# Mixture-of-experts stage on tokens sorted by expert, through DRAM, in place of all four experts on every token

## The chip, the cores and the metric

The kernel runs on one core of a Trainium2 chip. The metric is the device time of one execution in microseconds (us), lower is better. The engines are TensorE (PE, with its weight loads PEld), VectorE (DVE), ScalarE (ACT), GpSimd (POOL) and SyncE (SP); SP, ACT and POOL issue DMAs, which run on 16 shared DMA engines.

## The reference, cut to what matters

A residual stream `x` of 32 x 128 = 4096 tokens with 128 features passes through eight sublayers. Only the second half of the last one changes:

```python
x = x + mla_attention(rmsnorm(x, norm1_w), ...)
n = rmsnorm(x, norm2_w)
top = argmax(n @ gate_w.T + gate_b)                  # one expert of 4 for each token
h = relu(einsum('btd,ehd->bteh', n, W1) + b1)         # 128 -> 512 hidden
y = einsum('bteh,edh->bted', h, W2) + b2              # 512 -> 128
x = x + y[chosen expert]
```

All matmuls of these sublayers are in float32.

## The kernel before, in words

The program is a list of phases; every engine runs its own instruction list, and `phase_end` (line 971) is a barrier of all five engines after each phase. Within a phase, work is pipelined over the 32 items (an item is 128 tokens) with written-out lags (`steps`), and semaphores order the engines.

Phase 1 is the first attention, during which SP loads the weights of all layers (`late_loads`, line 2023). The phase "latent" (lines 1620 to 1760) makes queries, keys and values of the last attention, in two loops: 32 items with a 320-column matmul (line 1733), then 16 pairs. In the first loop ACT has three operations per item: `take_rows` (line 998), `take_z` (line 1697, the stream that goes on) and `take_latent` (line 1694). Phase "L4" is the last attention; POOL cuts the causal triangle out of the probabilities there (`cut`, line 518) and copies v (line 507).

The last phase is the expert stage, in 8 groups of 512 tokens. For each group: scale by the inverse root mean square (L1789), transposition (L1890), `norm2` (L1794), gate matmuls (L1896), the choice of the expert as a one-hot (L1804 to L1811). The one-hot is transposed and spread over partitions, so that each of four masks has a value per token (L1901, L1908, L1819). Then all four experts run on all 512 tokens: 16 chunks of "up" (L1916: weights 128x128, 512 moving columns), Relu with bias on ACT and DVE in turns (L1875, L1851), 16 chunks of "down" (L1938). DVE multiplies each expert's result by its mask and sums (`combine`, L1826, L1830); the sum is transposed back (L1922), added to the stream (L1837) and stored by SP (L2160). `up` runs two chunks ahead of `down`, and the next group's preparation is spread between the chunks, so that PE always has a matmul at hand:

```python
for c in range(CHUNKS):                               # 16
    ... nc.tensor.matmul(ps[:, 4 + e % 2, :], w_down[:, c, :], hid[:, c % 4, :], ...)
    if c + 2 < CHUNKS: up(i, k, c + 2)
```

## Time and profile before

| | us |
|---|---|
| median of 3 runs | 1413.96 (1412.5 to 1418.36) |
| span of the profiled execution | 1414.9 |
| PE busy / PEld busy | 1260.0 / 841.6 |
| DVE / ACT / POOL busy | 919.3 / 591.5 / 273.6 |
| expert stage, from L2171 to the last store | 1146.08 to 1414.9 |

The span runs from the first to the last instruction of one execution, which the profiler recorded; for that execution the profile gives no other time than this span. PE's matmuls are pipelined, so that the times from one start to the next say more than the durations of single instructions. A float32 matmul appears as two instructions.

### The profile page before, as it was taken

What the parts mean: (1) busy time and instruction counts of PE and PEld (TensorE: products, weight loads), DVE (VectorE), ACT (ScalarE), POOL (GpSimd) and SP (SyncE); (2) the same over time, 40 slices, a digit from 0 to 9 for tenths busy, and PEclk for the clock granted to TensorE, in tenths of its full rate; (3) what the DMA queues carried; (4) which work ended last, traced back from release to release, by engine and by line L of the source; (5) the groups of instructions that cost most, each with busy time, mean ns of one, the idle gap of its engine ahead of it and who ended that gap; (6) DMA issues with size and microseconds to landing.
All of it is one profiled execution on the core that took longest, in us unless ns stands there. A gap on an engine that the chain in (4) does not pass through costs nothing. (4 is left out here: it accounts for less than half of the span.)

```text
span 1414.9 us, 36612 instructions
## 1 busy us (share of the span) xinstructions
PE 1260.0 (89%) x13819; PEld 841.6 (59%) x13819; DVE 919.3 (65%) x2730; ACT 591.5 (42%) x1343; POOL 273.6 (19%) x766
## 2 busy tenths in 40 slices
PE   3999988938849997999898998799999959999998
PEld 2888876735437773444456886447888734444443
DVE  4778849976455875999423886756777645555554
ACT  2788845641234663222343554753444411111111
POOL 0222211220402330000000221434554500000000
PEclk9999998967977998999897999877999969999999
DMA  9500000000000003000000000010000000000000
GB/s 287 138 4 3 3 2 1 2 1 1 1 0 2 3 3 120 1 1 1 1 1 1 3 3 2 1 60 2 3 3 3 3 1 8 8 7 7 7 7 16
DMA packets 27076, 25.59 MB, mean 18 GB/s; under 512 B 6176, under 2 KB 22944, under 8 KB 26656
## 3 DMA queue, kind: packets, MB, share of 16 engines
q1 hardware_dynamic: 25904, 23.17, 5.5%
q8 instruction: 112, 1.84, 0.5%
q14 instruction: 52, 0.43, 0.1%
q10 hardware_dynamic: 1008, 0.16, 0.1%
HBM read 21.23 MB, written 2.10 MB: 16 GB/s over the span
## 5 line engine op out<-in xcount | busy, mean ns | idle before, releaser
L703 PE MATMUL ps<-kT,qTm 32*128 32x128 f32 x3200 | 252.4, 293 | 0.8 <-DVE kT L408 0.8
L671 PE MATMUL ps<-qTm,kT 32*128 32x512 f32 (+1 forms) x1024 | 250.8, 554 | 2.4 <-ACT probs L574 2.1
L703 PEld LDWEIGHTS ps<-kT,qTm 32*128 32x128 f32 x3200 | 228.3, 204 | 6.1 <-issue 2.6
L1938 PE MATMUL ps<-kv_all,ctx_all 128*128 128x512 f32 x256 | 134.1, 605 | 5.3 <-DVE kv_all L1851 5.3
L1875 ACT ACTIVATE kv_all<-ps,b_col 128x512 f32<-128x512 f32 x64 | 44.0, 687 | 215.9 <-PE ps L1916 215.9
L1916 PE MATMUL ps<-q_all,ctx_all 128*128 128x512 f32 x256 | 132.3, 599 | 0.0
L380 DVE TENSOR_REDUCE neg_max<-ps 128x8 f32<-128x1024 f32 x72 | 87.9, 1221 | 60.6 <-PE ps L703 60.6
L574 ACT ACTIVATE probs<-ps 128x1024 f32<-128x1024 f32 x72 | 73.7, 1024 | 121.0 <-PE ps L713 121.0
L1851 DVE TENSOR_SCALAR kv_all<-ps,b_col 128x512 f32<-128x512 f32 x64 | 48.0, 750 | 116.3 <-PE ps L1916 116.3
L860 PE MATMUL ps<-probs,v_wide 128*32 128x128 f32 x3200 | 116.9, 280 | 4.6 <-DVE o_sb L429 1.7
L671 PEld LDWEIGHTS ps<-qTm,kT 32*128 32x128 f32 x1024 | 85.5, 190 | 49.4 <-issue 40.2
L499 POOL CAST nm<-neg_max 128x16 bf16<-128x16 f32 (+1 forms) x132 | 26.8, 203 | 428.6 <-DVE neg_max L367 160.9
L375 DVE TENSOR_REDUCE neg_max<-ps 128x4 f32<-128x512 f32 x128 | 82.2, 684 | 33.2 <-PE ps L703 33.2
L394 DVE TENSOR_TENSOR qTm<-ps,hmask 128x512 f32<-128x512 f32 (+1 forms) x132 | 73.2, 555 | 37.7 <-ACT nmT L552 20.6
L713 PE MATMUL ps<-nmT,sel_max 32*128 32x128 bf16 x1600 | 95.9, 219 | 0.0
L570 ACT ACTIVATE probs<-ps,bias_col 128x512 f32<-128x512 f32 x128 | 80.9, 683 | 35.4 <-PE ps L713 35.4
L1529 PE MATMUL ps<-tap_w,xqT 128*128 128x512 f32 x192 | 93.6, 624 | 0.0
L860 PEld LDWEIGHTS ps<-probs,v_wide 128*32 128x32 f32 x3200 | 80.8, 111 | 19.6 <-issue 6.5
L1916 PEld LDWEIGHTS ps<-q_all,ctx_all 128*128 128x128 f32 x256 | 49.1, 192 | 61.3 <-issue 61.3
L564 ACT ACTIVATE probs<-ps,bias_col 128x1024 f32<-128x1024 f32 x64 | 71.3, 1114 | 32.5 <-PE ps L713 32.5
L827 PE MATMUL ps<-pv_pick,pv 128*128 128x72 f32 (+1 forms) x528 | 82.0, 278 | 0.9 <-ACT pv L580 0.9
L580 ACT ACTIVATE pv<-ps 128x256 f32<-128x256 f32 x132 | 50.6, 383 | 71.2 <-PE ps L860 71.2
(375 smaller groups left out, 2600.8 us busy)
## 6 DMA issues: line engine op xcount, KB each, us to landing
ctx_all<-in_ctx SPq DMA_DIRECT2D x4, 1024.0 KB, 10.5
ctx_all<-in_ctxT SPq DMA_DIRECT2D x2, 2048.0 KB, 10.5
x_all<-in_x SPq DMA_DIRECT2D x4, 512.0 KB, 7.0
out<-x_all SPq DMA_DIRECT2D x8, 256.0 KB, 2.3
ctx_all<-in_W1T SPq DMA_DIRECT2D x1, 1024.0 KB, 5.3
tap_w<-in_conv_wT SPq DMA_DIRECT2D x1, 768.0 KB, 7.0
w_l<-in_w SPq DMA_DIRECT2D x2, 256.0 KB, 3.4
above<-in_c_above SPq DMA_DIRECT2D x1, 256.0 KB, 3.4
```

The costliest lines, as they stand in the source:

```text
L375: nc.vector.tensor_reduce(neg_max[:, k, per * g:per * g + per], ps[:, raw_bank(L, b, g), 0:N].rearrange("p (h k) -> p h k", h=per), AX.X, ...
L380: nc.vector.tensor_reduce(neg_max[:, k, H2 * u:H2 * u + H2].rearrange("p (a h) -> p a h", a=2), ps[:, 4 * u:4 * u + 2, 0:N].rearrange("p a ...
L570: nc.scalar.activation(probs[:, k % 2, N * g:N * (g + 1)], ps[:, final_bank(L, b, g), 0:N], ACT.Exp, bias=bias).then_inc(sem("probs_ready" ...
L574: nc.scalar.activation(probs[:, k % 2, 2 * N * u:2 * N * (u + 1)].rearrange("p (a n) -> p a n", a=2), ps[:, 2:4, 0:N], ACT.Exp, bias=bias) ...
L671: nc.tensor.matmul(ps[:, bank, at:at + N], kT[rows_of(g), k, :], qTm[rows_of(g), k, 0:N], start=True, stop=False, skip_group_check=True)
L703: last = nc.tensor.matmul(dst, qTm[rows_of(g), k, 128 * i:128 * i + 128], kT[rows_of(g), k, :], start=False, stop=True, skip_group_check=True)
L713: last = nc.tensor.matmul(dst, sel_max[rows_of(g), i, :], nmT[rows_of(g), k, :], start=False, stop=True, skip_group_check=True)
L827: last = nc.tensor.matmul(ps[:, 7, 256 + W * half:256 + W * half + W], pv[:, k % 2, 128 * half:128 * half + 128], pv_pick[:, 0 if heads == ...
L860: last = nc.tensor.matmul(ps[32 * j:32 * j + 32, 7, 128 * half:128 * half + 128], v_tile(k % 2, heads, 4 * half + j, i), probs[:, k % 2, 1 ...
L1529: last = nc.tensor.matmul(dst, xqT[:, k % 2, tap:tap + 128], tap_w[:, tap, :], start=False, stop=tap == 2)
L1916: nc.tensor.matmul(ps[:, c % 2, :], w_up[:, c, :], xm_T[:, k, :], start=True, stop=True).then_inc(sem("mo_hidden"), 1)
L1938: nc.tensor.matmul(ps[:, 4 + e % 2, :], w_down[:, c, :], hid[:, c % 4, :], start=c % 4 == 0, stop=c % 4 == 3).then_inc(sem("mo_down"), 1)
```

## The change

The four experts no longer run on all tokens. In the latent phase the gate weights are appended to the 320-column weights as four more columns, and to the output projection of the last attention, so that the logits arrive in `z_all[:, b, 128:132]` beside the stream (one more small ACT copy per item). In L4 POOL also adds stream and residual into the right half of a record per token (`keep_rest`). A record has 257 words: normalised row, rest, token number.

The last phase then does this. DVE works out the expert, and a place for each token, from 20-odd small operations and two small matmuls. The places of one expert are consecutive, in a region of 4096 rows in a new DRAM tensor `places`. POOL scatters the 32 items' records to DRAM by 32 indirect DMAs of 128 records each. SP waits for all of them, and loads tiles of 512 records. Eleven tiles (8 + 3, enough for any split of the tokens) each run one expert, whose weights and biases (128 rows of 1156 words) POOL fetches by an indirect DMA. Four indirect DMAs per tile scatter the result rows of 512 B to the output; places without a token carry a number out of bounds, which is skipped. Tiles are held in 4 buffers, results and weights in 3. `places` (16,896 rows of 1028 B, 17.4 MB) is filled with empty records at the start, by one DMA of SP behind the loads of phase 1. Gone are the mask and its spreading, the constant `sel` (L1427), the loads of all experts (L2153) and the plain store.

The diff, cut to its core (in `mixture_vector` the choice and the places are left out; `mixture_*` take the places of `expert_*` and `store`):

```diff
+TILE_ROWS = 512
+N_TILES = B * S // TILE_ROWS + N_EXP3 - 1
+TILE_SLOTS = 16
+RECORD = 2 * D + 1
+REGION = B * S
+SPARE = N_EXP3 * REGION
+NO_TOKEN = 1 << 20
+EXPERT_ROW = 2 * HID + HID // 128 + D
...
+            def keep_rest(b, k):
+                pool.wait_ge(*after("x_updated", b + 1))
+                nc.gpsimd.tensor_tensor(records[:, b, D:2 * D], x_all[:, b, :], z_all[:, b, 0:D], ALU.add)
...
+            if L == "L4":
+                work += [(9, keep_rest)]
...
-            nc.scalar.activation(sel[:], sel_col[:].unsqueeze(2).broadcast_to([128, 16, 128]), ACT.Copy)
...
-            nc.scalar.activation(w_h1[:], w_h1[:], ACT.Copy, scale=col("norm1")).then_inc(sem("la_weights"), 1)
-            act.wait_ge(sem("la_centred"), 1)
-            nc.scalar.activation(w_h1[:], ps[:, 6, 0:320], ACT.Copy).then_inc(sem("la_weights"), 1)
+            nc.scalar.activation(w_h1[:, 0:320], w_h1[:, 0:320], ACT.Copy, scale=col("norm1")).then_inc(sem("la_weights"), 1)
+            nc.scalar.activation(w_h1[:, 320:320 + N_EXP3], gate_w[:], ACT.Copy, scale=col("norm2")).then_inc(sem("la_weights"), 1)
+            act.wait_ge(sem("la_centred"), 2)
...
             def take_latent(b, k):
                 act.wait_ge(sem("la_halves"), b + 1)
+                nc.scalar.activation(z_all[:, b, D:Z], ps[:, 2 + k, 320:320 + N_EXP3], ACT.Copy, scale=inv_ln[:, b:b + 1])
...
-            nc.tensor.matmul(ps[:, 6, 0:320], centre[:], w_h1[:], start=True, stop=True).then_inc(sem("la_centred"), 1)
+            pe.wait_ge(sem("la_weights"), 2)
+            nc.tensor.matmul(ps[:, 7, 0:N_EXP3], w_o3_nat[:], w_h1[:, 320:320 + N_EXP3], start=True, stop=True
+                             ).then_inc(sem("la_centred"), 1)
+            nc.tensor.matmul(ps[:, 6, 0:320 + N_EXP3], centre[:], w_h1[:], start=True, stop=True
+                             ).then_inc(sem("la_centred"), 1)
...
                 wait_reuse(pe, after("la_raw"), b, RING)
-                nc.tensor.matmul(ps[:, 2 + k, 0:320], rowT[:, k % 2, :], w_h1[:], start=True,
+                nc.tensor.matmul(ps[:, 2 + k, 0:320 + N_EXP3], rowT[:, k % 2, :], w_h1[:], start=True,
...
+        def stored_after(engine, j):
+            if j >= 0:
+                engine.wait_ge(sem("mx_stored_%d" % (j % 3)), 64 * (j // 3 + 1))
+        def mixture_sync(sp):
+            sp.wait_ge(sem("mx_tiled"), 1)
+            for j in range(N_TILES):
+                row = sp.value_load(tile_row[0:1, j:j + 1], min_val=0, max_val=SPARE)
+                if j == 0:
+                    sp.wait_ge(sem("mx_placed_rows"), 16 * B)
+                stored_after(sp, j - 4)
+                sp.dma_start(tile_of(j), places[bass.ds(row, TILE_ROWS), :].rearrange("(k p) c -> p k c", p=128)
+                             ).then_inc(sem("mx_loaded_%d" % (j % 4)), 16)
+            for j in range(N_TILES - 3, N_TILES):
+                stored_after(sp, j)
+        def mixture_gpsimd(pool):
+            G = nc.gpsimd
+            G.memset(restart, 1.0).then_inc(sem("mx_restart"), 1)
+            G.tensor_copy(records[:, :, 2 * D:RECORD].bitcast(I32), token_id[:].unsqueeze(2)).then_inc(sem("mx_ids"), 1)
+            pool.wait_ge(sem("mx_restart"), 1)
+            G.memset(by_expert(restart)[:, :, 0:1], 0.0).then_inc(sem("mx_restart"), 1)
+            def fetch(j):
+                G.indirect_dma_start(out=expert_of(j), out_offset=None, in_=t_in["experts"],
+                                     in_offset=bass.IndirectOffsetOnAxis(ap=weight_id[:, j:j + 1], axis=0)
+                                     ).then_inc(sem("mx_weights_%d" % (j % 3)), 16)
+            pool.wait_ge(sem("mx_ids"), 1)
+            pool.wait_ge(sem("places_cleared"), 16)
+            pool.wait_ge(sem("mx_placed"), 1)
+            for b in range(B):
+                pool.wait_ge(sem("mx_rows"), b + 1)
+                G.indirect_dma_start(out=places, out_offset=bass.IndirectOffsetOnAxis(ap=place_id[:, b:b + 1], axis=0),
+                                     in_=records[:, b, :], in_offset=None).then_inc(sem("mx_placed_rows"), 16)
+                if b == 8:
+                    pool.wait_ge(sem("mx_tiled"), 1)
+                    for j in range(3):
+                        fetch(j)
+            for j in range(N_TILES):
+                pool.wait_ge(sem("mx_result"), j + 1)
+                for k in range(4):
+                    G.indirect_dma_start(out=out_rows_2d, out_offset=bass.IndirectOffsetOnAxis(
+                                             ap=tile_of(j)[:, k, 2 * D:RECORD].bitcast(I32), axis=0),
+                                         in_=result_of(j)[:, 128 * k:128 * k + 128], in_offset=None,
+                                         bounds_check=B * S - 1, oob_is_err=False
+                                         ).then_inc(sem("mx_stored_%d" % (j % 3)), 16)
+                if j + 3 < N_TILES:
+                    fetch(j + 3)
...
+        def mixture_scalar(act):
+            act.wait_ge(sem("mx_inv"), 1)
+            for b in range(B):
+                nc.scalar.activation(records[:, b, 0:D], z_all[:, b, 0:D], ACT.Copy, scale=inv_all[:, b:b + 1]
+                                     ).then_inc(sem("mx_rows"), 1)
+            for j in range(N_TILES):
+                relu_free(act, j)
+                for c in (0, 2):
+                    act.wait_ge(sem("mx_up"), 4 * j + c + 1)
+                    nc.scalar.activation(hidden_of(j, c), ps[:, 2 + c, :], ACT.Relu, bias=b_up(j, c)
+                                         ).then_inc(sem("mx_relu_even"), 1)
...
+            def take_features(j):
+                dve.wait_ge(sem("mx_turned"), j + 1)
+                if j >= 2:
+                    dve.wait_ge(sem("mx_up"), 4 * (j - 1))
+                V.tensor_scalar(features_of(j), ps[:, j % 2, :], col("norm2"), None, ALU.mult
+                                ).then_inc(sem("mx_features"), 1)
+            def relu(j):
+                relu_free(dve, j)
+                for c in (1, 3):
+                    dve.wait_ge(sem("mx_up"), 4 * j + c + 1)
+                    V.tensor_scalar(hidden_of(j, c), ps[:, 2 + c, :], b_up(j, c), 0.0, ALU.add, ALU.max
+                                    ).then_inc(sem("mx_relu_odd"), 1)
+            def add_bias(j):
+                rest = tile_of(j)[:, :, D:2 * D]
+                q.count(V.tensor_tensor(rest, rest, b_down(j).unsqueeze(1).broadcast_to([128, 4, D]), ALU.add))
+            def finish(j):
+                dve.wait_ge(sem("mx_down"), j + 1)
+                stored_after(dve, j - 3)
+                q.end()
+                V.tensor_tensor(result_of(j).rearrange("p (k d) -> p k d", k=4),
+                                ps[:, 6 + j % 2, :].rearrange("p (k d) -> p k d", k=4), tile_of(j)[:, :, D:2 * D], ALU.add
+                                ).then_inc(sem("mx_result"), 1)
+            take_features(0)
+            take_features(1)
+            relu(0)
+            for j in range(N_TILES):
+                add_bias(j)
+                if j + 2 < N_TILES:
+                    take_features(j + 2)
+                if j + 1 < N_TILES:
+                    relu(j + 1)
+                finish(j)
...
+            pe.wait_ge(sem("mx_chosen"), 1)
+            nc.tensor.matmul(ps[:, 0, 0:128], upperb[:], one_hot, start=True, stop=True)
+            nc.tensor.matmul(ps[:, 1, 0:128], onesb[:], one_hot, start=True, stop=True).then_inc(sem("mx_counted"), 1)
+            def turn(j):
+                pe.wait_ge(sem("mx_loaded_%d" % (j % 4)), 16 * (j // 4 + 1))
+                if j >= 2:
+                    pe.wait_ge(sem("mx_features"), j - 1)
+                for k in range(4):
+                    last = nc.tensor.transpose(ps[:, j % 2, 128 * k:128 * k + 128], tile_of(j)[:, k, 0:D], ident[:])
+                last.then_inc(sem("mx_turned"), 1)
+            def up(j):
+                pe.wait_ge(sem("mx_features"), j + 1)
+                pe.wait_ge(sem("mx_weights_%d" % (j % 3)), 16 * (j // 3 + 1))
+                for c in range(4):
+                    if j:
+                        pe.wait_ge(sem("mx_relu_odd" if c % 2 else "mx_relu_even"), 2 * (j - 1) + c // 2 + 1)
+                    nc.tensor.matmul(ps[:, 2 + c, :], w_up(j, c), features_of(j), start=True, stop=True
+                                     ).then_inc(sem("mx_up"), 1)
+            def down(j):
+                pe.wait_ge(sem("mx_relu_even"), 2 * j + 2)
+                pe.wait_ge(sem("mx_relu_odd"), 2 * j + 2)
+                if j >= 2:
+                    pe.wait_ge(sem("mx_result"), j - 1)
+                for k in range(4):
+                    for c in range(4):
+                        last = nc.tensor.matmul(ps[:, 6 + j % 2, 128 * k:128 * k + 128],
+                                                hidden_of(j, c)[:, 128 * k:128 * k + 128], w_down(j, c),
+                                                start=c == 0, stop=c == 3)
+                last.then_inc(sem("mx_down"), 1)
+            turn(0)
+            turn(1)
+            up(0)
+            for j in range(N_TILES):
+                if j + 2 < N_TILES:
+                    turn(j + 2)
+                if j + 1 < N_TILES:
+                    up(j + 1)
+                down(j)
...
+            sp.wait_ge(sem("empty_set"), 2)
+            sp.dma_start(places.rearrange("(p r) c -> p r c", p=128),
+                         empty_row[:].unsqueeze(1).broadcast_to([128, (SPARE + TILE_ROWS) // 128, RECORD])
+                         ).then_inc(sem("places_cleared"), 16)
...
-        def expert_loads(sp):
-            sp.dma_start(w_up.rearrange("p (e c) h -> p e (c h)", e=N_EXP3), t_in["W1T"].rearrange("e d n -> d e n")).then_inc(sem("experts_loaded"), 16)
-            sp.dma_start(w_down, t_in["W2T"].rearrange("e (c h) d -> h (e c) d", h=128)).then_inc(sem("experts_loaded"), 16)
-            sp.wait_ge(sem("experts_loaded"), 32)
```

## Rows read from the trace of the kernel before

**Rows 1.** First lines of the profile's page: busy us, share, instructions.

```profile
span 1414.9 us, 36612 instructions
PE 1260.0 (89%) x13819; PEld 841.6 (59%) x13819; DVE 919.3 (65%) x2730; ACT 591.5 (42%) x1343; POOL 273.6 (19%) x766
```

**Rows 2.** A stretch of the expert stage: length, busy time of each engine, clock, DMA.

```profile
1250.00:1300.00 50.00, 48.09 (x157) 23.27 (x156) 27.62 (x56) 8.24 (x12) 2.53 (x2) 1.00 0.04 10
```

**Rows 3.** Groups by line in the expert stage: busy us, mean ns, idle before.

```profile
L1938 PE MATMUL ps<-kv_all,ctx_all 128*128 128x512 f32 x256 | 134.1, 605 | 5.3 <-DVE kv_all L1851 5.3
L1916 PE MATMUL ps<-q_all,ctx_all 128*128 128x512 f32 x256 | 132.3, 599 | 0.0
...
L1851 DVE TENSOR_SCALAR kv_all<-ps,b_col 128x512 f32<-128x512 f32 x64 | 48.0, 750 | 116.3 <-PE ps L1916 116.3
...
L1830 DVE TENSOR_TENSOR kv_all<-kv_all 128x512 f32<-128x512 f32 x24 | 16.6, 692 | 4.0 <-DVE kv_all L1826 3.4
```

**Rows 4.** Chain of waits, expert stage: start, us, engine, line, count.

```profile
1301.87 0.86 PE ps L1916 x2
```

**Rows 5.** Timeline, end of L4 and expert stage: start, us, engine, line, idle before.

```profile
1142.49 0.29 DVE L436 TENSOR_TENSOR ctx_all<-ctx_all,ps 128x128 f32<-128x128 f32 x1 [0.95 <-PE ps L783]
...
1145.76 0.19 DVE L241 SCALAR_TENSOR_TENSOR inv_all<-moment,inv_all 128x32 f32<-128x32 f32 x1
...
1157.74 3.59 PE L1916 MATMUL ps<-q_all,ctx_all 128*128 128x512 f32 x4
...
1164.60 0.60 PE L1890 MATMUL ps<-ident,kv_all 128*128 128x128 f32 x4
...
1168.47 0.95 PE L1896 MATMUL ps<-gate_w,q_all 128*128 128x4 f32 x8
```

**Rows 6.** DMA issues: size, median us from issue to landing.

```profile
x_all<-in_x SPq DMA_DIRECT2D x4, 512.0 KB, 7.0
out<-x_all SPq DMA_DIRECT2D x8, 256.0 KB, 2.3
ctx_all<-in_W1T SPq DMA_DIRECT2D x1, 1024.0 KB, 5.3
```

**Rows 7.** Timeline of SP's DMA issues at the start: start, us, count.

```profile
5.36 9.75 SPq L2019 DMA_DIRECT2D ctx_all<-in_ctx  x4
...
35.25 0.42 SPq L2029 DMA_DIRECT2D above<-in_c_above  x1
...
70.90 0.59 SPq L2029 DMA_DIRECT2D cols<-in_ln_b  x1
```

**Rows 8.** Timeline of the latent phase's first loop.

```profile
895.05 0.25 ACT L1694 ACTIVATE ctx_all<-ps 128x64 f32<-128x64 f32 x1
895.15 0.31 ACT L998 ACTIVATE rowT<-ps 128x128 f32<-128x128 f32 x1
...
895.71 0.25 ACT L1694 ACTIVATE ctx_all<-ps 128x64 f32<-128x64 f32 x1
...
915.97 1.43 ACT L1708 ACTIVATE o_sb<-ctx_all 128x64 f32<-128x64 f32 x4 [1.61 <-DVEq L1658]
```

**Rows 9.** POOL's timeline in L4, and its adder in the latent phase.

```profile
895.21 0.46 POOL L1675 TENSOR_TENSOR q_all<-probs 128x128 f32<-128x128 f32 x1 [0.19 <-DVE ctx_all L1633]
...
1043.40 1.09 POOL L518 TENSOR_SCALAR_AFFINE_SELECT probs<-probs 128x1024 f32<-128x1024 f32 x1 [0.41 <-PE ps L776]
...
1046.64 0.20 POOL L499 CAST nm<-neg_max 128x16 bf16<-128x16 f32 x1 [2.15 <-DVE neg_max L380]
```

**Rows 10.** Two early stretches, columns as in Rows 2.

```profile
20.00:35.00 15.00, 11.01 (x79) 8.92 (x81) 6.59 (x13) 5.67 (x20) 0.57 (x3) 1.00 1.07 304
...
50.00:70.00 20.00, 20.00 (x422) 17.49 (x420) 15.76 (x34) 16.79 (x44) 4.81 (x20) 1.00 0.46 122
```

**Rows 11.** Timeline, the end of phase 1, and the copy of `sel`.

```profile
201.54 0.21 DVE L220 TENSOR_TENSOR moment<-stats_all 128x32 f32<-128x32 f32 x1 [0.43 <-SPq L971]
...
393.11 1.89 ACT L1427 ACTIVATE sel<-sel_col 128x2048 bf16<-128x2048 f32 x1
```

More of the change, by code:

```diff
@@ L121, with build @@
 BIASES = ("L0", "L2", "L3")
-def build(nc, t_in, out):
+TILE_ROWS = 512
[6 more added lines that the diff above has]
+EXPERT_ROW = 2 * HID + HID // 128 + D
+def build(nc, t_in, out, places):
     with ExitStack() as ctx_:
@@ L1768, in build @@
-        chosen = work_m[:, 4096:8192].rearrange("p (k e t) -> p k e t", k=2, e=4)
-        xm_T = q_all[:, 0:8, :].rearrange("p a b -> p (a b)").rearrange("p (k t) -> p k t", k=2)
-        def loop_groups(engine, body):
-            body(0, 0)
-            with engine.Fori(0, GROUPS // 2 - 1) as pair:
-                for u in range(2):
-                    body(pair * 2 + (u + 1), (u + 1) % 2)
-            body(GROUPS - 1, 1)
-        def is_last(i):
-            return isinstance(i, int) and i == GROUPS - 1
@@ L1869, in expert_scalar @@
-        def expert_scalar(act):
-            def group(i, k):
-                for c in range(0, CHUNKS, 2):
-                    act.wait_ge(sem("mo_hidden"), i * CHUNKS + (c + 1))
-                    if c >= 4 or not is_first(i):
-                        act.wait_ge(sem("mo_down"), i * CHUNKS + (c - 3))
-                    nc.scalar.activation(hid[:, c % 4, :], ps[:, c % 2, :], ACT.Relu,
-                                         bias=b1_col[:, c:c + 1]).then_inc(sem("mo_relu_even"), 1)
-            loop_groups(act, group)
@@ L2282, in constants @@
     up, none = np.arange(1, SLOTS + 1), np.full(SLOTS, -1)
-    sel = np.zeros((128, 16))
-    for i in range(16):
-        sel[3 * i:3 * i + 3, i] = sel[64 + 3 * i:64 + 3 * i + 3, i] = 1
     row = t % 32
@@ L2346 @@
     out = nc.dram_tensor("out_0", (B, S, D), F32, kind="ExternalOutput").ap()
-    build(nc, t_in, out)
+    places = nc.dram_tensor("places", (SPARE + TILE_ROWS, RECORD), F32).ap()
+    build(nc, t_in, out, places)
     got = run_bass_kernel_spmd(nc, [{"in_" + n: a for n, a in arrays.items()}], core_ids=[0])
```

306 lines of the change are left out of this document (118 added, 188 removed).

## The prediction, made before the changed kernel ran

> **What bounds the kernel now.** I read the page's first lines, then the busy time by stretches, then the groups by line of the last phase, then its timeline. The page gives a span of 1414.9 us with PE busy for 89% of it [rows 1]. In the expert stage PE is the only engine without slack: in a 50 us stretch it is busy 48.09 us at full clock, DVE 27.62 and ACT 8.24 [rows 2]. The groups by line say with what: 266.4 us of summed durations are the 128 "up" and 128 "down" matmuls [rows 3]. One matmul of 512 columns takes 0.86 us of PE from start to start (its two instructions) [rows 4], so 256 of them are 220 us of the 268.9 us from the end of the moments, 1145.95 us [rows 5], to the end of the span. No DMA ends a wait there. The stage is bound by matmul work of which three quarters are masked away.
>
> **What the change takes away.** All of that stage: 268.9 us. What it puts in its place is a prologue that PE only waits for, and eleven tiles. I build the new end from 1145.95 us, within the profiled execution.
>
> **Side costs before the stage.** In the latent loop ACT starts the same operation every 0.66 us (895.05, 895.71), back to back, so it has no room [rows 8]. The added copy of four columns has the form of L1694, which holds the next one up by 0.10 us (895.05 to 895.15); from above, the copies with scale and bias take 1.43/4 = 0.36 us each [rows 8]. I take 0.17, nearer to the like row, since a scale per partition comes with it: 32 x 0.17 = 5.4 us (3.2 to 11.5). The two small copies and the small matmul ahead of the loop I put at 0.7 us. POOL's `keep_rest` is a 128x128 add, 0.46 us [rows 9], in a step of L4 with gaps of 0.41 and 2.15 us on POOL; the cut behind it is then late by some 0.1 us, and its reader on PE runs a step later. Hidden; only the last one shows at the barrier, 0.4 us. If that cover were gone, it costs 32 x 0.46 = 15 us. The four more columns in L4's products cost nothing that can be seen. Dropping the copy of `sel` gains between 0 and its 1.89 us [rows 11]; I take 0. Together +6.5: the stage starts at 1152.5 us.
>
> **The cleared places.** 17.4 MB are written from about 71.5 us, behind the last load [rows 7]. At the 304 GB/s of the loads at 20 to 35 us [rows 10] that is 57 us; at the 114 GB/s that 256 KB landing in 2.3 us give [rows 6], 153 us, to 224 us. The first barrier that SP shares falls at about 201.5 us [rows 11]. So it costs 0 down to 135 GB/s, and 23 us at worst. PE was busy all through 50 to 70 us with the DMA engines 46% busy [rows 10], so I put instruction fetches beside the clearing at 0, 10 us at worst.
>
> **Routing.** Seven DVE operations, each waiting for the one before, two small matmuls, seven more. A 128x128 operation takes 0.29 us, one of 32 elements 0.19 [rows 5]; with the gaps between them 2.3 + 0.9 + 2.3 = 5.5 us. At 1158.0 the first scatter can go; ACT's 32 records started at 1152.5, at about 0.4 us each, and stay ahead.
>
> **POOL's indirect DMAs** are the number that decides, and the trace before has none. Call X what one takes on POOL. From below: SP's plain issue, 0.42 us [rows 7]. From above: the issues of 1 MB each that SP could only pass on as the DMA engines took them, 9.75/4 = 2.44 us [rows 7]. A store of 256 KB lands 2.3 us after its issue [rows 6], so a DMA of half of that takes at most 1.15 us at that rate if only the data count. POOL has to work out 128 addresses one by one, which SP needn't; I take the middle, X = 1.4.
>
> The Trainium skill ("DMA: Bandwidth & Descriptors", anatomy of one DMA on the SWDGE path) puts a DMA from GpSimd at about 2.0 us + bytes/436e3, most of it the receipt of the write and little the descriptors. For 131.6 KB that is, as an estimate from that page, 2.3 us, which agrees with the 2.3 us of the store's row; if it held POOL for all that time, the end would be at 1184 + 87 x 2.3 = 1384 us (the line of the rivals below); if the receipts overlap, it speaks for a small X.
>
> 32 scatters and the 3 weight fetches among them are 35 X = 49 us: to 1207.0. The last scatter lands 2.3 us later, SP issues the first load (0.45) and 526 KB land in 3.7 us (between 2.3 for 256 KB and 7.0 for 512 KB under load [rows 6], near the 5.3 of 1 MB): 1213.5. No other engine has work in these 55 us.
>
> **The tiles.** On PE one tile is 4 transpositions, 0.48 us (4 in 0.60 with the last one's drain [rows 5]), 4 "up" at 0.86 = 3.4, and 16 "down" of 128 columns, 32 instructions with a weight load each: the gate matmuls, with the same loads and almost no columns, show 0.95/8 = 0.12 us each [rows 5], so 3.8 us. That is 7.7 us against DVE's 0.75 for features, 2 x 0.75 for Relu, 0.69 for the bias and 0.75 for the result [rows 3], which are 3.7. If the weight loads don't hide, 32 x 0.19 = 6.1, and 10.0 us a tile.
>
> POOL needs 5 X = 7.0 us a tile. But two rings are longer than either. Tile j+4 is loaded when tile j's rows are stored: three PE tiles from its transposition to its result, 23.1 + 0.9, 4 X = 5.6, landing 2.3, issue and load 4.15, together 36 us for 4 tiles, 9.0 each. The weights of tile j+3 are fetched after the four scatters of tile j: 5 X = 7.0, landing 4.3, and 15.8 us on PE until the next result, 27.1 for 3 tiles, 9.0 each. I take 9.0.
>
> From the first load to the first result: two sets of transpositions, features, waiting for the second load, "up" at half clock for its first part (four instructions, two matmuls, took 3.59 us after the idle start at 1157.74 [rows 5], against 2 x 0.86 later), the second "up", "down", result: 17 us, to 1230.5. Ten more tiles: 1320.5. Four scatters 5.6, landing 2.3, end 0.3: 1328.7. The span of 1414.9 stands 0.9 above the median of the runs; less that, **1328 us**, 86 less than before.
>
> **The rivals.**
> *X small (0.6).* POOL is then never the last. Scatter 21 us, tiles at 8.0 us by the load ring: 1158 + 21 + 6.5 + 17 + 80 + 2.4 + 2.6 = 1288 us. For it: the wait of a DMA is no work of the issuer, SP's 0.42. Against it: the scatters' data alone, at 1.15 us each, would then end last. Chance 0.12.
> *X from 1.9 to 2.5.* POOL bounds the tiles too (5 X over 9): what doesn't hang on X is 1158 + 6.5 + 17 + 2.6 = 1184, and all 87 indirect DMAs (32 + 11 + 44) stand in a row: 1184 + 87 X, at 2.2 1375 us. For it: SP's 2.44 under full queues. Chance 0.15.
> *Slower: POOL becomes the bound altogether.* The same line crosses 1415 at X = 2.65; at 3.0 the time is 1445. It takes one mechanism: each indirect DMA holds POOL until its 128 descriptors are written and taken, one after the other. For it: nothing in the trace shows POOL doing this quickly, and all 87 stand on the path. Against it: above every row that I have. Chance 0.08.
> *The clearing holds phase 1.* 23 us more, 1351 us, if the DMA engines write these rows below 135 GB/s. Chance 0.05.
>
> The Trainium skill ("SBUF — State Buffer", the box on DVE blocking DMA) says that descriptors from GpSimd wait while DVE runs an operation that takes both ports. [...] No row here shows it.
>
> **How the numbers follow.** Forecast (X of 0.9 to 1.9, 1304 to 1357) 0.60, the rivals as above. No change needs X within a tenth of 2.65. Within 0.5% (7 us) is what a measurement of this kernel can't tell from no change. Faster 0.87, same 0.03, slower 0.10. The range goes from the small X, 1288, to POOL-bound tiles at X = 2.45, 1397.
>
> **What would show it.** Right: the time from the first scatter to the first tile load about 50 us with PE idle; tiles every 9 us, PE idle in each for 1 to 2 us behind a DMA; the latent loop at about 0.83 us an item. Wrong: tiles every 5 X with PE waiting for `mx_loaded` throughout (POOL is the bound), or every 7.7 us (the rings are shorter than I think); PE waiting at the first barrier for SP; a "down" above 4 us. The forecast falls with X: every 0.1 us in it is 5 to 9 us.

## The result, and the profile after

The changed kernel takes 1375.2 us (median of 4 runs, 1372.5 to 1377.4); the kernel before took 1415.3 us beside it (4 runs, 1412.5 to 1418.4). The ratio is 0.972, with a 95% interval of 0.970 to 0.974: faster by 40 us, where 86 had been forecast. The time lies in the range, and the likeliest case was wrong by 47 us.

The page's first lines, which answer to [rows 1]: PE is busy for 137 us less, and the span is only 39.5 us shorter.

```profile
span 1375.4 us, 35566 instructions
PE 1122.9 (82%) x13531; PEld 797.6 (58%) x13531; DVE 834.0 (61%) x2554; ACT 577.8 (42%) x1366; POOL 362.8 (26%) x882
```

**Phase 1.** The timeline of DVE at the end of phase 1 and the list of DMA issues (size, us to landing). The first line answers to the one at 201.54 us in [rows 11]: the phase ends 36.4 us later. DVE was released there by SP's queue with only 0.43 us of idle time, as before; nobody stood at the barrier waiting for the clearing.

```profile
237.91 0.21 DVE L227 TENSOR_TENSOR moment<-stats_all 128x32 f32<-128x32 f32 x1 [0.43 <-SPq L993]
...
places<-empty_row SPq DMA_DIRECT2D x1, 16962.0 KB, 92.1
```

Three stretches of the changed kernel, columns as in [rows 2]: two beside the clearing, one behind it. The second line of [rows 10] has 422 matmuls in 20 us, 21 a microsecond; here there are 12 to 14, PE is idle for 22 to 27% of the time, and the granted clock is 0.83 to 0.85. The DMA engines are busy all the time.

```profile
72.00:100.00 28.00, 20.41 (x343) 17.17 (x345) 13.87 (x30) 14.51 (x36) 3.60 (x15) 0.85 1.05 194
...
130.00:165.00 35.00, 27.44 (x447) 22.66 (x437) 17.42 (x36) 18.68 (x47) 6.09 (x25) 0.83 0.91 175
165.00:200.00 35.00, 35.00 (x690) 30.18 (x689) 25.74 (x55) 27.25 (x69) 9.03 (x39) 0.92 0.01 3
```

What PE waited for there is in its timeline. All nine idle times of PE beside the clearing, 20.8 us in sum, end on "issue": no semaphore and no other engine released them. Four of the nine:

```profile
85.24 1.22 PE L717 MATMUL ps<-kT,qTm 32*128 32x128 f32 x9 [4.58 <-issue]
97.15 0.44 PE L841 MATMUL ps<-pv_pick,pv 128*128 128x72 f32 x2 [3.01 <-issue]
106.50 0.38 PE L717 MATMUL ps<-kT,qTm 32*128 32x128 f32 x2 [1.46 <-issue]
115.06 0.92 PE L874 MATMUL ps<-probs,v_wide 128*32 128x128 f32 x22 [2.66 <-issue]
```

The nine fall on five different lines of the program, so no one operation causes them. What they have in common is the number of PE's instructions between them. Cut at these starts, the stretches hold the same number of matmuls and of weight loads each (columns as above; four of the eight):

```profile
85.24:97.15 11.91, 8.90 (x123) 7.68 (x123) 5.22 (x10) 5.49 (x12) 1.20 (x5) 0.72 1.11 207
97.15:106.50 9.35, 7.89 (x123) 6.59 (x123) 5.17 (x11) 5.04 (x13) 1.21 (x5) 0.82 1.12 199
106.50:115.06 8.56, 5.90 (x122) 4.88 (x123) 5.32 (x11) 5.27 (x12) 2.18 (x9) 1.00 1.11 207
...
143.06:152.22 9.16, 8.97 (x123) 7.54 (x123) 4.37 (x9) 4.48 (x11) 1.21 (x5) 0.63 1.09 203
```

That is 123 and 123 in every one of the eight stretches (122 to 124 by the records): PE stops after a fixed number of its own instructions. This points at the fetch of the next block of its program, which comes late: one block every 9.4 us on average (75.6 us for the eight), where at 21 matmuls a microsecond PE uses up a block in 5.9. How fast PE works through a block doesn't change the distance much: at a granted clock of 1.00 it is 8.56 us with a long stop, at 0.63 it is 9.16 us with almost none. So the lower clock costs little of its own.

The lists of DMA queues from 70 to 200 us, before and after the change, have the packets of an instruction queue:

```profile
q8 instruction: 21, 0.34, 1.1%
...
q8 instruction: 16, 0.26, 0.9%
```

A packet has 16 KB, and in both kernels PE issues some 240 matmuls and weight loads from 72 to 200 us for each packet of that time. So this queue carries PE's program, and beside the clearing fewer blocks came.

**The stage.** `inv_all` is ready at 1184.86 us, against the 1145.95 of [rows 5]; without phase 1's 36.4 that is 2.5 us later, not 6.5. POOL's timeline where the record scatters end, then SP's loads and PE's first transposition:

```profile
1233.54 0.96 POOL L1872 DMA_INDIRECT places<-kv_flat,place_id  x1 [0.30 <-issue]
1234.81 0.96 POOL L1872 DMA_INDIRECT places<-kv_flat,place_id  x1 [0.30 <-issue]
1237.77 3.88 SPq L1851 DMA_DIRECT2D kv_flat<-places  x4
1241.61 1.11 PE L1999 MATMUL ps<-ident,kv_flat 128*128 128x128 f32 x4 [53.53 <-DMA kv_flat<-places]
```

From start to start a scatter takes POOL 1.27 us: X, which had been put at 1.4. The DMAs' landings, which answer to [rows 6]:

```profile
kv_flat<-places SPq DMA_DIRECT2D x11, 514.0 KB, 4.8
out<-kv_flat POOLq DMA_INDIRECT x44, 2.3
places<-kv_flat,place_id POOLq DMA_INDIRECT x32, 2.8
ctx_all<-in_experts,weight_id POOLq DMA_INDIRECT x11, 4.5
```

**The tiles** come in pairs. The timeline of a pair and the start of the next: POOL's L1881 is the first scatter of a result, PE's L1999 the transposition, L2008 up, L2018 down, DVE's L1975 the result.

```profile
1267.04 1.00 POOL L1881 DMA_INDIRECT out<-kv_flat  x1 [1.29 <-DVE kv_flat L1975]
...
1270.57 1.12 PE L1999 MATMUL ps<-ident,kv_flat 128*128 128x128 f32 x4 [5.06 <-DMA kv_flat<-places]
...
1271.48 5.98 PE L2008 MATMUL ps<-kv_flat,ctx_all 128*128 128x512 f32 x8
...
1277.29 3.73 PE L2018 MATMUL ps<-ctx_all,probs 128*128 128x128 f32 x32
...
1281.30 3.60 PE L2008 MATMUL ps<-kv_flat,ctx_all 128*128 128x512 f32 x8
...
1282.55 1.00 POOL L1881 DMA_INDIRECT out<-kv_flat  x1 [9.35 <-DVE kv_flat L1975]
...
1289.99 1.00 POOL L1881 DMA_INDIRECT out<-kv_flat  x1 [1.29 <-DVE kv_flat L1975]
...
1293.70 1.12 PE L1999 MATMUL ps<-ident,kv_flat 128*128 128x128 f32 x4 [5.24 <-DMA kv_flat<-places]
```

1289.99 - 1267.04 = 22.95 us for two tiles. In every second one PE waits 5 us for a load, and the up behind the wait takes 5.98 us instead of 3.60: its clock has fallen (0.87 on average from 1260 to 1350).

### The profile page after: what moved, and what is told of

The parts are those of the page before. It is cut to its first block and busy times, and to the rows that moved or that the text cites. A ratio compares the mean times of both kernels' runs of the same rounds, so it can differ in the third digit from the quotient of the medians.

```text
span 1375.4 us, 35566 instructions
## 1 busy us (share of the span) xinstructions
PE 1122.9 (82%) x13531; PEld 797.6 (58%) x13531; DVE 834.0 (61%) x2554; ACT 577.8 (42%) x1366; POOL 362.8 (26%) x882
## 5 line engine op out<-in xcount | busy, mean ns | idle before, releaser
L717 PE MATMUL ps<-kT,qTm 32*128 32x128 f32 x3200 | 261.2, 299 | 9.1 <-issue 8.3
L685 PE MATMUL ps<-qTm,kT 32*128 32x512 f32 (+1 forms) x1024 | 257.6, 568 | 3.3 <-ACT probs L588 1.6
L717 PEld LDWEIGHTS ps<-kT,qTm 32*128 32x128 f32 x3200 | 236.4, 210 | 15.4 <-issue 12.1
L874 PE MATMUL ps<-probs,v_wide 128*32 128x128 f32 x3200 | 121.8, 286 | 10.4 <-issue 5.8
L387 DVE TENSOR_REDUCE neg_max<-ps 128x8 f32<-128x1024 f32 x72 | 87.9, 1221 | 60.1 <-PE ps L717 60.1
L874 PEld LDWEIGHTS ps<-probs,v_wide 128*32 128x32 f32 x3200 | 83.5, 113 | 27.1 <-issue 14.3
L841 PE MATMUL ps<-pv_pick,pv 128*128 128x72 f32 (+1 forms) x528 | 83.8, 282 | 3.9 <-issue 3.0
L496 POOL COPY nm<-bias 128x12 bf16<-128x12 bf16 x96 | 18.9, 201 | 255.7 <-SPq L993 242.1
L374 DVE TENSOR_REDUCE neg_max<-ps 128x8 f32<-128x1024 f32 x64 | 77.9, 1217 | 2.2 <-PE ps L717 2.0
L841 PEld LDWEIGHTS ps<-pv_pick,pv 128*128 128x128 f32 x528 | 71.6, 197 | 12.4 <-issue 5.9
L727 PEld LDWEIGHTS ps<-nmT,sel_max 32*128 32x128 bf16 x1600 | 72.3, 97 | 10.6 <-issue 8.3
L430 DVE RECIPROCAL inv_den<-ps 128x16 f32<-128x16 f32 (+1 forms) x132 | 30.3, 230 | 74.3 <-PE ps L841 70.7
## 6 DMA issues: line engine op xcount, KB each, us to landing
places<-empty_row SPq DMA_DIRECT2D x1, 16962.0 KB, 92.1
ctx_all<-in_ctxT SPq DMA_DIRECT2D x2, 2048.0 KB, 10.4
```

Source lines behind the costliest of these rows:

```text
L374: nc.vector.tensor_reduce(neg_max[:, k, 0:heads].rearrange("p (a h) -> p a h", a=2), ps[:, pair:pair + 2, 0:2 * N].rearrange("p a (h k) -> ...
L387: nc.vector.tensor_reduce(neg_max[:, k, H2 * u:H2 * u + H2].rearrange("p (a h) -> p a h", a=2), ps[:, 4 * u:4 * u + 2, 0:N].rearrange("p a ...
L685: nc.tensor.matmul(ps[:, bank, at:at + N], kT[rows_of(g), k, :], qTm[rows_of(g), k, 0:N], start=True, stop=False, skip_group_check=True)
L717: last = nc.tensor.matmul(dst, qTm[rows_of(g), k, 128 * i:128 * i + 128], kT[rows_of(g), k, :], start=False, stop=True, skip_group_check=True)
L727: last = nc.tensor.matmul(dst, sel_max[rows_of(g), i, :], nmT[rows_of(g), k, :], start=False, stop=True, skip_group_check=True)
L841: last = nc.tensor.matmul(ps[:, 7, 256 + W * half:256 + W * half + W], pv[:, k % 2, 128 * half:128 * half + 128], pv_pick[:, 0 if heads == ...
```

## The experiments

All times are medians; where runs were compared, the kernel before was timed on the same chip beside them, at 1413.4 to 1414.5 us.

**1. The clearing taken out of phase 1.** Regions of 4608 places, and SP clears what a tile can read beyond an expert's records, once the counts are known:

```
-REGION = B * S
+REGION = B * S + TILE_ROWS
...
-            sp.dma_start(places.rearrange("(p r) c -> p r c", p=128),
-                         empty_row[:].unsqueeze(1).broadcast_to([128, (SPARE + TILE_ROWS) // 128, RECORD])
-                         ).then_inc(sem("places_cleared"), 16)
...
+            clear(slice(SPARE, SPARE + TILE_ROWS))
+            sp.wait_ge(sem("mx_placed"), 2)
+            for e in range(N_EXP3):
+                end = sp.value_load(end_row[0:1, e:e + 1], min_val=REGION * e, max_val=REGION * e + B * S)
+                clear(bass.ds(end, TILE_ROWS))
```

> The 17.4 MB clearing in phase 1 is gone; instead SP clears, during the routing and the scatters, the 512 rows behind each expert's last record and the 512 spare rows (2.6 MB in five DMAs). Theory A (the clearing held up the engines' instruction fetches in phase 1): phase 1 ends at 201 to 204 us as before the change (the changed kernel: 237.9), PE shows no idle time on issue in it, clock 1.00; the whole 1375 - 36 = 1339 us (1335 to 1345). Rival B (phase 1 grew for another reason, such as the new layout or the memsets): phase 1 still ends near 238 and the whole stays at 1370 to 1378. Rival C (2.6 MB beside the scatters slow POOL's indirect DMAs): phase 1 as in A, but one scatter takes over 1.5 us instead of 1.27, the whole 1347 to 1360.

Measured: 1342.2 us (1339.4 to 1346.7), ratio to before 0.949 (0.946 to 0.953): 33 us less than the changed kernel. The end of phase 1 and a stretch of it, in this kernel's timeline and its table of stretches:

```profile
201.29 0.22 DVE L227 TENSOR_TENSOR moment<-stats_all 128x32 f32<-128x32 f32 x1 [0.44 <-SPq L994]
...
100.00:130.00 30.00, 30.00 (x625) 26.14 (x624) 23.54 (x50) 24.96 (x64) 8.04 (x34) 1.00 0.01 3
```

PE is never idle, 21 matmuls a microsecond again. Theory A holds, B falls. C falls too: a scatter still takes 1.27 us, though its rows land after 6.1 us (median) and not 2.8 beside the 2.6 MB.

**2. Half the bytes.** Regions of 2048 places:

```
-REGION = B * S
+REGION = B * S // 2
```

> Regions of 2048 places in place of 4096 (enough for this input, not for any), so the same one DMA clears half the bytes, 8.9 MB; nothing else changes. Theory A (fetches wait behind the clearing for as long as it runs): half the clearing, half the loss: it lands after about 47 us, phase 1 ends at about 220 us, the whole 1357 us (1353 to 1362). Rival B (the loss doesn't hang on the bytes): 1370 to 1378. Rival C (the barrier waits for the clearing's end, or only its last part hurts): phase 1 as short as before, 202, the whole 1339.

Measured: 1366.4 us (1363.0 to 1366.6), 24 us above experiment 1 where the whole clearing costs 33. That is more than half, and 9 us above the forecast of A. In this trace phase 1 ends at 228.2 us, 26.9 later than in experiment 1. The list of DMA issues and PE's timeline show why: half the bytes took 56.2 us, and not the 47 that A had put, and there are five stops for five blocks, 10 us apart.

```profile
places<-empty_row SPq DMA_DIRECT2D x1, 8738.0 KB, 56.2
...
83.24 1.08 PE L874 MATMUL ps<-probs,v_wide 128*32 128x128 f32 x14 [4.95 <-issue]
93.48 0.71 PE L717 MATMUL ps<-kT,qTm 32*128 32x128 f32 x9 [0.53 <-issue]
104.25 0.70 PE L841 MATMUL ps<-pv_pick,pv 128*128 128x72 f32 x2 [4.60 <-issue]
114.41 0.37 PE L717 MATMUL ps<-kT,qTm 32*128 32x128 f32 x2 [2.00 <-issue]
124.54 1.00 PE L874 MATMUL ps<-probs,v_wide 128*32 128x128 f32 x22 [2.84 <-issue]
```

How long the clearing runs sets how many blocks come late, and each costs 4.4 us here (10.3 between two starts instead of 5.9). The 10.3 is no matter of the half: in the traces of experiments 4 to 8, which have the whole clearing (96 to 98 us there), a block takes 9.9 to 10.4 us, and the 9.4 above is the fastest of all. In all these traces the stops stand at the same places of the program in the same order (L874, L717, L841, L717, L874 and on), whatever the time: PE stops at fixed places of its instruction list.

**3. The same clearing, whole, in another phase.** The DMA moves behind the two loads of `ctxT`, which SP issues later; with phase 1 short it goes out at 544.06 us and not at 574.

```
                 sp.dma_start(ctxT[:, c, :, :], t_in["ctxT"][128 * c:128 * c + 128]).then_inc(sem("ctxT_loaded"), 16)
+            sp.wait_ge(sem("empty_set"), 2)
+            sp.dma_start(places.rearrange("(p r) c -> p r c", p=128),
...
```

> The same 17.4 MB clearing in one DMA, issued behind the two ctxT loads at 574 us instead of at 72 us: it then runs to about 680 us beside a phase in which PE is 97% busy with 4 instructions a us (phase 1: 21 a us). Theory A (what the clearing holds up is the fetch of instructions): phase 1 ends at 201 as before the change, the later phase loses a fifth of the 36 us at most, 0 to 7 us; the whole 1342 to 1349 us. Rival B (the clearing slows engines that work beside it, whatever their instructions are, by the 40% seen in phase 1): the later phase loses about 36 us, the whole stays at 1372 to 1380.

Measured: 1341.4 us (1340.1 to 1346.6), the time of experiment 1. The clearing now takes 104.4 us, and this is what two stretches beside it look like:

```profile
560.00:600.00 40.00, 39.07 (x163) 18.26 (x163) 37.29 (x153) 8.82 (x21) 0.00 (x0) 1.00 1.12 189
600.00:640.00 40.00, 38.89 (x163) 18.15 (x162) 37.15 (x155) 8.76 (x20) 0.00 (x0) 1.00 1.10 198
...
places<-empty_row SPq DMA_DIRECT2D x1, 16962.0 KB, 104.4
```

With the DMA engines as full as in phase 1, PE keeps its clock and its pace, and no idle time ends on "issue". It issues 4 matmuls a microsecond, so that 123 of them last 30 us, three times what a block takes to come. B falls: it is not the traffic alone that slows the engines, but the need for new instructions beside it. The upper end of A's range (7 us) wasn't needed either.

**4. Deep rings.** Eight tile buffers and six weight buffers:

```
-            at = EXPERT_ROW * (j % 3)
+            at = EXPERT_ROW * (j % 6)
...
-            at = 4 * RECORD * (j % 4)
+            at = 4 * RECORD * (j % 8)
...
-                stored_after(sp, j - 4)
+                stored_after(sp, j - 8)
...
+            for j in range(3, 6):
+                fetch(j)
...
-                if j + 3 < N_TILES:
-                    fetch(j + 3)
+                if j + 6 < N_TILES:
+                    fetch(j + 6)
```

> The clearing stays. Eight tile buffers in place of four (results and features move to q_all) and six weight buffers in place of three. Theory A (the rings close over two tiles, since PE's transposition of tile j+4 stands ahead of the down products of tile j+2): PE waits no more for tile loads after the first, its clock stays at 1.00, tiles come every 8.0 us instead of 11.3 (bounds 7.7 to 8.6), the whole 1375 - 22 = 1353 us (1346 to 1358). Rival B (POOL's five indirect DMAs of a tile or the loads' rate set the pace): period 11 us still, 1372 to 1378. Rival C (PE's products themselves are slow in this stage): PE busy throughout, period above 9.5, 1362 to 1370.

Measured: 1348.4 us (1345.0 to 1353.2), 27 us less, a little more than expected. The first scatters of two results that follow each other, in POOL's timeline, and a stretch among the tiles:

```profile
1281.74 1.00 POOL L1891 DMA_INDIRECT out<-q_all,kv_flat  x1 [1.28 <-DVE q_all L1985]
...
1289.18 1.00 POOL L1891 DMA_INDIRECT out<-q_all,kv_flat  x1 [1.28 <-DVE q_all L1985]
...
1275.00:1305.00 30.00, 30.00 (x178) 22.17 (x177) 14.01 (x21) 5.50 (x8) 19.99 (x21) 1.00 0.51 165
```

A tile takes 7.44 us, with PE busy throughout at full clock. That is the PE-bound time that the prediction had as 7.7.

**5 to 7. Which ring, and why.** One execution each: only the tile buffers (5), only the weight buffers (6), and PE's order with the buffers as they were (7), whose edit is

```
-                if j + 2 < N_TILES:
-                    turn(j + 2)
                 if j + 1 < N_TILES:
                     up(j + 1)
                 down(j)
+                if j + 2 < N_TILES:
+                    turn(j + 2)
```

> The changed kernel with eight tile buffers alone; the weight buffers stay three. This splits the two rings. Theory A (either ring closes over two tiles: weights of tile j+3 are fetched behind the four scatters of tile j, 5 x 1.28 = 6.4 us, land after 4.5, and up of tile j+3 stands ahead of down of tile j+2, 3.6 + 3.7 + 0.75): the weight ring is 19 us for two tiles, period 9.5 us, PE waits for ctx_all (weights) in every second tile, the whole about 1375 - 18 = 1357 us. Rival B (the tile ring was the only one): period 7.4 us as with both rings deep, the whole about 1346.

> The changed kernel with six weight buffers and three more weight fetches behind the scatters; tile buffers stay four. Theory A (the tile ring is the longer one): nothing gained, the pairs stay, period 11 us, and the three fetches beside the first loads delay the first result by about 3 us: 1375 to 1380. Rival B (the weight ring was the one that bound): period about 7.5, 1350.

> The changed kernel, only that PE's transposition of tile j+2 stands behind the down products of tile j and not ahead of them; buffers as they were. Theory A (the tile ring closed over two tiles because of this place in PE's order): it closes over three now, 22 us for three tiles; the weight ring of two tiles (10.1 us a tile in the run with eight tile buffers) is then what is left, plus about 1 us for the features that PE now waits for: period 10 to 10.5 us instead of 11.3, PE waits for kv_flat<-places only at the first tile, the whole 1375 - 10 = 1365 us (1360 to 1370). Rival B (the order doesn't matter, the number of buffers does): PE still waits 5 us for kv_flat<-places in every second tile, 1373 to 1379.

Eight tile buffers: 1369.1 us where A forecast 1357, a miss in the size; in pairs still, 1283.36 - 1263.15 = 20.2 us for two tiles, 10.1 each (9.5 expected). Six weight buffers: 1376.1 us, pairs of 23 us, nothing gained, as expected. One execution also carries what went before the stage, so I compare the time from `inv_all` to the end: 190.5 us in the changed kernel, 163.0 in experiment 4, 178.3 with eight tile buffers and 191.8 with six weight buffers. So the tile ring is the longer, the weight ring is right behind it, and to deepen one alone gives 12 us or nothing of the 27. With eight tile buffers the wait stands before up, which needs the weights; the trace names no releaser for it:

```profile
1272.89 5.37 PE L2013 MATMUL ps<-q_all,ctx_all 128*128 128x512 f32 x8 [3.39 <-issue]
```

Here "issue" fits another cause than in phase 1: the weights' DMA of tile 3 was issued at 1268.32, such a DMA takes 4.5 us to land (median), and up starts at 1272.89.

PE's other order took the waits for tile loads away (54.7 us in 2 times, the first tile's, where the changed kernel has 76.1 in 6), as theory A said. But the time went up to 1384.8 us, where A forecast 1365: a miss. A pair takes 1295.90 - 1272.31 = 23.6 us. On DVE, `finish(j)` stands behind `take_features(j + 2)`, and this waits for the transposition that I had moved back. The timeline shows the result 3 us behind the end of down instead of 1:

```profile
1279.68 3.73 PE L2018 MATMUL ps<-ctx_all,probs 128*128 128x128 f32 x32
1283.25 0.60 PE L1999 MATMUL ps<-ident,kv_flat 128*128 128x128 f32 x4
1283.89 0.75 DVE L1957 TENSOR_SCALAR kv_flat<-ps,cols 128x512 f32<-128x512 f32 x1 [11.78 <-PE ps L1999]
...
1285.87 0.68 DVE L1975 TENSOR_TENSOR kv_flat<-ps,kv_flat 128x512 f32<-128x512 f32 x1
```

So the ring that is left, the weights', grew by 2 us, and up behind the wait takes 6.3 to 6.5 us instead of 5.4. I had looked at what the move does on PE and not at what waits behind it on DVE.

**8. What an indirect DMA costs POOL.** The record scatters of half the rows:

```
-                G.indirect_dma_start(out=places, out_offset=bass.IndirectOffsetOnAxis(ap=place_id[:, b:b + 1], axis=0),
-                                     in_=records[:, b, :], in_offset=None).then_inc(sem("mx_placed_rows"), 16)
+                G.indirect_dma_start(out=places, out_offset=bass.IndirectOffsetOnAxis(ap=place_id[0:64, b:b + 1], axis=0),
+                                     in_=records[0:64, b, :], in_offset=None).then_inc(sem("mx_placed_rows"), 16)
```

> The changed kernel, but each of the 32 record scatters sends only the rows of partitions 0 to 63 (half the records are left out, so half of the tokens get no result). It tells what an indirect DMA costs POOL. Theory A (a fixed cost for one DMA): still 1.27 us from start to start, the whole 1375 +- 3. Rival B (POOL works through its rows one by one): 0.96 falls to about 0.5 and the period to 0.8 us, the scatters take 15 us less, the whole about 1360.

Measured, in one execution: 1378.0 us, a scatter every 1.20 us. In the group of POOL, 0.90 us of one for 64 rows against 0.97 for 128:

```profile
L1872 POOL DMA_INDIRECT places<-kv_flat,place_id x32 | 28.9, 904 | 18.3 <-ACT kv_flat L1897 9.5 <-issue 8.8
```

X is fixed but for 0.07 us in 64 rows; theory A. To save POOL's time one must issue fewer DMAs, not shorter ones.

**9. Both causes removed.** Experiments 1 and 4 together.

> Both: the ends cleared in place of all places, eight tile and six weight buffers. If both causes are right and add up: 1375 - 36 - 22 = 1317 us (1308 to 1325), which would be the best kernel. If they overlap or one falls: 1335 or more.

Measured: 1316.1 us (1312.5 to 1321.2), ratio 0.932 (0.929 to 0.935). 33 + 27 = 60 from the single ones, 59 together: they add up.

**10 to 12. What is left of the start.** Three steps on top of it. Experiment 10 (`e11_best` in the expectations): five weight buffers with the fourth fetched among the scatters, up of the first tile ahead of the second transposition, and ten matmuls on PE before the tile comes. Experiment 11 (`e12_sp_weights`, e12 for short): the weights by SP, with plain DMAs whose address is in a register. Experiment 12: another release of the matmuls.

> The ends cleared, eight tile buffers, five weight buffers of which the fourth is fetched among the scatters (not three more behind them), the first up ahead of the second transposition, and ten matmuls of no use on PE while it waits for the first tile, so that its clock is up when the tile arrives. Against the kernel with ends and deep rings (1316 us): fetches no longer compete with the first loads (3 us), the first up doesn't wait for the second load (2.7 us) and runs at full clock (2.4 us): 1308 us (1304 to 1313). If the clock falls again before the tile arrives or the ten matmuls delay the tile: 1311 to 1318.

> Against e11_best: SP fetches the weights of a tile with plain DMAs from an address in a register (five buffers), so that POOL issues 76 indirect DMAs and not 87; three loads go out ahead of the other five; eight matmuls of no use on PE in place of ten, from POOL's last scatter on. If an indirect DMA costs POOL 1.27 us wherever it stands, the four among the scatters go off the path: 1312.8 - 5 - 1 = 1307 us (1302 to 1310). If SP's register loads or the shared queue delay the first tile by as much: 1311 to 1316.

> As e12_sp_weights, but the eight matmuls of no use are released by a small memset that POOL executes between its last two scatters. In e12 they were released by a semaphore step of POOL's sequencer and ran at 1177 to 1189 us, 8 us ahead of POOL's last scatter, so that PE was cold again (up of the first tile 6.74 us) when the tile came at 1203. Theory A (POOL's sequencer runs ahead of the queue of its indirect DMAs, an executed instruction doesn't): they run beside the last scatter's landing and the load, up of the first tile takes 3.7 us, and the whole is 3 us shorter: 1302 us (1299 to 1305). Rival B (the memset costs POOL, or the matmuls end after the tile has come): 1304 to 1308.

```
+            pe.wait_ge(*fetched(3))
+            for n in range(10):
+                nc.tensor.matmul(ps[:, 7, :], ident[:], x_all[:, 0:4, :].rearrange("p a b -> p (a b)"),
+                                 start=True, stop=True)
             turn(0)
-            turn(1)
             up(0)
+            turn(1)
...
+                    at = sp.value_load(weight_id[0:1, j:j + 1], min_val=0, max_val=128 * (N_EXP3 - 1))
+                    sp.dma_start(expert_of(j), t_in["experts"][bass.ds(at, 128), :]).then_inc(fetched(j)[0], 16)
...
-                    pool.sem_inc(sem("mx_restart"), 1)
+                    G.memset(q_flat[:, 3584:3588], 0.0).then_inc(sem("mx_restart"), 1)
```

Measured: 1312.8 us (1310.4 to 1316.3), 1304.7 us (1302.5 to 1310.1) and 1304.3 us (1299.2 to 1306.6). The first gave 3 us of the 8 hoped for: its matmuls ended at 1208.6, 6.6 us behind SP's issue of the load, and the transposition ran only then. The second gave 8, a little more than forecast, with 11 indirect DMAs fewer. In the stage alone (from `inv_all` to the end) it is 5.0 us, 160.1 to 155.1, and the scatters, with four fetches fewer among them, take 39.5 us from the first start to the last instead of 44.6. The third gave nothing that can be measured (154.6 us in the stage). Its matmuls did move to the right place, the first up took 3.70 us instead of 6.74, but they ended later than the tile had come: the transposition ran 6.8 us after the load's issue, and 4.0 in experiment 11. What the clock gave, they took: rival B.

```profile
1188.58 0.12 POOL L1907 MEMSET q_all<- 128x4 f32 x1
1188.75 9.95 PE L2057 MATMUL ps<-x_all,ident 128*128 128x512 f32 x16 [42.71 <-POOL q_all L1907]
1188.89 0.97 POOL L1908 DMA_INDIRECT places<-kv_flat,place_id  x1 [0.19 <-issue]
1191.75 9.46 SPq L1876 DMA_DIRECT2D kv_flat<-places  x8
1198.54 0.60 PE L2032 MATMUL ps<-ident,kv_flat 128*128 128x128 f32 x4
```

Experiments 11 and 12 are the fastest, at ratios of 0.9225 (0.920 to 0.925) and 0.9224 (0.920 to 0.925) to the kernel before: 110 us less, against 40 for the change as it stood.

## Why the prediction was wrong

By the profiled execution, from the sum of 1328.7 us to the 1375.4 measured:

| step | forecast | measured | difference |
|---|---|---|---|
| clearing, at the end of phase 1 | 0 | 36.4 | +36.4 |
| other costs before the stage | 6.5 | 2.5 | -4.0 |
| routing, to the first scatter | 5.5 | 6.6 | +1.1 |
| 35 indirect DMAs | 49 | 44.3 | -4.7 |
| to the first result | 23.5 | 23.0 | -0.5 |
| ten more tiles | 90 | 101.6 | +11.6 |
| last result to the end | 8.2 | 15.0 | +6.8 |

*The clearing: the step that failed.* The prediction had "PE was busy all through 50 to 70 us with the DMA engines 46% busy [rows 10], so I put instruction fetches beside the clearing at 0, 10 us at worst". The reading of the row was right and carries no further than 46%: the clearing kept the DMA engines full. I looked for its price at the barrier (the rival of 23 us, with PE waiting for SP), and it stands nowhere near: experiments 1 to 3 show 33 us for it, all of it in PE's own stream, in the phase with the most instructions, and none in a phase that needs few.

The Trainium skill ("Runtime: NRT & Kernel Launch", instruction fetch mechanics) says that an engine's program is streamed in blocks of 256 instructions, 16 KiB each, over a DMA queue of the sequencer's own. The trace agrees with the block (packets of 16 KB; 123 matmuls and 123 weight loads between two stops, so that 10 of 256 would be others, which the view doesn't count). The Trainium skill calls the crossing mostly hidden; here it isn't, 9.4 us a block beside the clearing, and the measurement decides. That the fetches wait behind the clearing's packets inside the DMA engines is the likely way, but only argued: the traces show that fewer packets came, and not the time at which each was asked for.

*The tile ring: the other step that failed.* "Tile j+4 is loaded when tile j's rows are stored: three PE tiles from its transposition to its result", 36 us for four tiles. The terms were about right; the ring was drawn wrong. PE takes its instructions in order, and the transposition of tile j+4 stands ahead of the down products of tile j+2. So the load that waits for tile j holds up the result of tile j+2 already: from the scatters' start at 1259.60 to SP's issue 6.3 us, load 4.7, transposition 0.9, up 5.8, down 3.8, result and POOL's start 1.5: 23.0 us for two tiles, and again from there. The weight ring closes in the same way over two tiles and not three (experiment 5). What the sum did not have either is the clock: it fell in each wait of 5 us, and up took 2.4 us longer behind the wait shown above (5.98 us and 3.60). Experiment 4 gives back 27 us.

*The end* was 6.8 us longer, by two things. The last tile's result follows the one before after 3.6 us, when POOL, at 1.29 us a DMA, still has two scatters of the older one ahead: 7.2 us to its last issue, where 5.6 were put down. From the end of that issue to the end of the span it is 7.7 us, and the landing, 2.3 us from the start of a scatter, is over after 1.3 of them. SP's queue shows the rest: it waits for the drain that POOL executes at the end of its program (L993), for 5.9 us. The sum had 0.3.

```profile
SPq L133 <- POOLq L993: 5.9, 1, 5.9
```

*What held.* X, the number that the sum hung on, was 1.27 and inside its bounds of 0.42 and 2.44 near the value taken. That is luck in part: 1.4 was the middle of two bounds from plain DMAs, and the reason given for it, 128 addresses worked out one by one, does not hold, since 64 rows fewer save 0.07 us (experiment 8). It is chance, too, that the rival with X = 2.2 names 1375 us, the time measured; its mechanism is not in the trace. The case that POOL bounds the tiles (5 X = 6.4 under 7.4) did not come. PE's tile is 7.44 (7.7). The latent loop, at 0.79 us an item from 0.66, cost 0.13 x 32 = 4 of the 5.4 forecast; the stage as a whole began 2.5 us late, and between executions of the experiments this start differs by more than that (1142.8 to 1151.1 in the five without the large clearing). `keep_rest` stayed hidden. A price of DVE's work on POOL's descriptors did not show: an indirect DMA takes 1.29 us among the tiles, where DVE works, and 1.27 among the scatters.

## What to carry to other kernels

A large DMA of no haste is not free because its engine waits for nothing: before placing it, count the instructions that the busiest engine issues per microsecond beside it, and put it where they are few (17.4 MB cost 33 us beside 21 matmuls a microsecond and nothing beside 4). To find the length of a ring of buffers, walk it in the order in which each engine takes its instructions; an operation that waits for the buffer and stands early in that order closes the ring early, and two rings of nearly one length must be widened together. An indirect DMA costs POOL nearly the same for 64 rows as for 128 (1.20 and 1.27 us), so where POOL is on the path, what can go out as a plain DMA with a register address belongs on another queue (experiment 11). And a time that agrees with a rival's forecast says nothing for its mechanism until a trace has shown the mechanism's own number.

## What had not been expected of the hardware

- PE stops on "issue" after 123 matmuls and 123 weight loads each time (122 to 124 by the records) while the DMA engines are full, 8.6 to 11.9 us from start to start in the eight stretches.
- POOL's sequencer runs ahead of its indirect DMAs: in experiment 11 a semaphore step that stands ahead of the last scatter in POOL's program released PE's matmuls at 1180.90 us, 15 us ahead of that scatter (1196.29), with 13 scatters still to start. They were done at 1189.49. (The expectation of experiment 12 puts their start at 1177.) A memset in the same place (experiment 12) was executed 0.3 us ahead of the scatter.

```profile
1180.90 8.59 PE L2057 MATMUL ps<-x_all,ident 128*128 128x512 f32 x16 [27.35 <-POOLq L1907]
```

- Behind the last indirect DMA POOL's drain held the end for 5.9 us; the kernel before, with no DMA on POOL, ended 2.4 us after its last issue on SP. In experiment 11, with eight tile buffers, it was 5.1 us, and 1305.4 - 1298.6 = 6.8 us from the last scatter to the end (7.7 in the changed kernel). What the drain waits for the trace doesn't show.
- One clearing of 16962 KB in rows of 1028 bytes from SBUF to DRAM took 92.1 and 104.4 us, 166 to 189 GB/s; loads of 514 KB of the same rows ran at 350 GB/s in experiment 9, eight at once.
